# Retention: the gate multiplies the result right after its squares, the root's factor last; one half gets row buffers of its own

## The reference

```python
q, k, v = heads(query, W_Q), heads(key, W_K), heads(value, W_V)      # 16 heads of 32
q, k = xpos(q), xpos(k, downscale=True)
ret = einsum(einsum(q, k) * decay_mask, v)
mu, var = ret.mean(-1), ret.var(-1)                                  # over the 32 of a head
ret = (ret - mu) / sqrt(var + 1e-5)
gate = silu(query @ g_w.T + g_b)
x = layernorm(query + ret * gate @ out_w.T + out_b)
```

## Time and profile before

| | us |
|---|---|
| median of 3 runs | 1864.24 |
| range | 1863.15 to 1866.96 |
| the profiled execution's own time | 1863.1 |
| its span, first to last instruction | 1861.3 |
| TensorE busy over the span | 1696.8 |
| DVE, ACT, POOL busy | 1392.4, 1053.7, 1056.4 |

### The profile page before, as it was taken

How to read it: one execution, slowest core, us unless ns; L and a number is a source line. 1 busy time by engine, 2 the same in 40 slices (tenths; PEclk the granted TensorE clock), 3 DMA queues, 4 the chain that set the end, 5 groups by cost and what they waited for, 6 DMA issues and landing times. The chain is left out here.

```text
span 1861.3 us, 37218 instructions
## 1 busy us (share of the span) xinstructions
PE 1696.8 (91%) x13426; PEld 764.8 (41%) x13426; DVE 1392.4 (75%) x3069; ACT 1053.7 (57%) x1865; POOL 1056.4 (57%) x999
## 2 busy tenths in 40 slices
PE   5898999989999999998787899999999997799897
PEld 2433343433433344333233455545455553344343
DVE  7687756786677866678654977878778777688798
ACT  5346655675556655566642556555465454465587
POOL 4049867687685967869862664645655555000054
PEclk9999999999999999999897999999999999899999
DMA  8302112231113211212224223322232221561085
GB/s 274 116 17 60 55 29 58 70 93 42 24 50 95 88 35 37 74 54 78 86 86 157 70 81 98 112 84 91 85 108 76 75 92 57 189 236 48 23 315 188
DMA packets 125263, 172.27 MB, mean 93 GB/s; under 512 B 24600, under 2 KB 75160, under 8 KB 124184
## 3 DMA queue, kind: packets, MB, share of 16 engines
q1 hardware_dynamic: 119704, 161.37, 27.0%
q10 hardware_dynamic: 5376, 8.52, 1.4%
HBM read 106.38 MB, written 38.14 MB: 78 GB/s over the span
## 5 line engine op out<-in xcount | busy, mean ns | idle before, releaser
L1153 DVE CUSTOM_DVE_ANT_0 a_mx<-a_mx,a_mqk 128x128 f32<-128x128 f32 (+3 forms) x512 | 241.9, 512 | 131.2 <-PE a_mx L1353 130.4
L963 ACT ACTIVATE a_P<-a_mx 128x512 f32<-128x512 f32 (+3 forms) x441 | 199.7, 498 | 148.7 <-PE a_mx L1371 79.7
L1236 POOL TENSOR_TENSOR a_P<-a_P 128x512 f32<-128x512 f32 (+3 forms) x202 | 194.0, 987 | 107.9 <-PE a_o L1383 95.3
L1367 PE MATMUL a_mx<-a_Qs,a_Ks 128*128 128x512 f16 (+3 forms) x768 | 231.2, 334 | 17.3 <-ACT a_P L963 5.5
L1353 PE MATMUL a_mx<-a_Ks,a_Qs 96*128 96x512 f16 (+3 forms) x768 | 227.2, 332 | 10.7 <-DVE a_nm L1153 3.9
L963 ACT ACTIVATE share<-a_mx 128x512 f32<-128x512 f32 (+3 forms) x327 | 145.4, 492 | 107.4 <-PE a_mx L1371 59.6
L1236 POOL TENSOR_TENSOR a_P<-a_P,share 128x512 f32<-128x512 f32 (+3 forms) x199 | 184.3, 955 | 27.9 <-ACT share L963 17.4
L1156 DVE TENSOR_REDUCE a_nm<-a_mx 128x1 f32<-128x512 f32 x256 | 164.7, 684 | 30.9 <-PE a_mx L1353 30.0
L2217 PE MATMUL r_pj<-share,cth 128*128 128x512 f16 x672 | 172.6, 391 | 6.9 <-PEq L123 5.5
L2937 PE MATMUL f_pj<-f_xqT,f_wgu 128*128 128x512 bf16 x704 | 158.3, 381 | 2.3 <-ACT f_sg L2779 2.3
L2217 PE MATMUL r_pj<-r_xTh,share 128*128 128x512 f16 x512 | 157.9, 381 | 2.6 <-DVE r_xTl L2064 1.7
(11 more groups left out here) (294 smaller groups left out, 4027.1 us busy)
## 6 DMA issues: line engine op xcount, KB each, us to landing
x_scratch<-rows SPq DMA_DIRECT2D x60, 256.0 KB, 2.0
rows<-x_scratch SPq DMA_DIRECT2D x56, 256.0 KB, 4.5
lead<-in_xT SPq DMA_DIRECT2D x24, 512.0 KB, 4.6
lead<-in_ctxT SPq DMA_DIRECT2D x38, 256.0 KB, 2.8
h_scratch<-f_h SPq DMA_DIRECT2D x3, 2816.0 KB, 9.2
f_h<-h_scratch SPq DMA_DIRECT2D x3, 2816.0 KB, 14.3
a_Ks<-a_kph SPq DMA_DIRECT2D x256, 32.0 KB, 1.9
a_Qs<-a_qph SPq DMA_DIRECT2D x256, 32.0 KB, 1.9
```

What stands on the lines that cost most here:

```text
L963: act.activation(Pf[pf.at[key]][:, off:512], pb[:, off:512], ACT.Exp).then_inc(p_exp, 1)
L1153: dve.tensor_tensor_reduce(bank_of(it)[:, 0:n], bank_of(it)[:, 0:n], mqk[:, 512 - n:512], 1.0, -3e38, ALU.add, ALU.max, nm[:, col:col + 1] ...
L1236: pool.tensor_tensor(total[:, off:512], total[:, off:512], Pf[pf.at[key]][:, off:512], ALU.add).then_inc(add_pool, 1)
L1367: m = pe.matmul(pb[:, off:512], Ks[s][:, j, kt * P:(kt + 1) * P], Qs[s][:, j, qb * 512 + off:(qb + 1) * 512], start=True, stop=not diag)
```

## The change

1. `zg` is now the multiplication of `r_rt` by the gate. DVE does it (into one of two buffers `r_zt`) as soon as `sq` has read the result and the gate is there. The multiplication by the root's factor `r_rex` comes last, on POOL, in place in `r_zt` (item `z.0`). One multiplication on DVE and one on POOL for each unit, as before.
2. The gate's buffer and R's bank are free after `zg` (R's also needs `sq`), no longer after the last multiplication; the plan's conditions say the same.
3. The last but one half, `AHEAD = (3, 0)`, keeps its rows in four buffers of its own, `r_ahead`. The last half uses `rows`, which half (2, 1) left earlier. Its loads are put 2.1 places earlier in the plan.

```diff
@@ retention_plan
-            put("ACT", ("G", *u), 1.9, out, lambda: was("z", n - 2))
+            put("ACT", ("G", *u), 1.9, out, lambda: was("zg", n - 2))
...
-            put("ACT", ("sq", *u), 0.54, lambda: put("DVE", ("var", *u), 1.3, var), lambda: was("rt", n - 1))
+            put("ACT", ("sq", *u), 0.54, lambda: (done.add(("sq", *u)), put("DVE", ("var", *u), 1.3, var), put(
+                "DVE", ("zg", *u), 0.62, gated, lambda: has(("G", *u)) and was("zl", n - 2))), lambda: was("rt", n - 1))
...
-                "DVE", ("rt", *u), 0.65, rt, lambda: was("zg", n - 1)))))
+                "DVE", ("rt", *u), 0.65, rt, lambda: was("z", n - 1)))))
+
+        def gated():
+            done.add(("zg", *u))
...
-            put("POOL", ("zg", *u), 1.4, gated, lambda: has(("G", *u)))
-
-        def gated():
-            done.add(("zg", *u))
-            put("DVE", ("z", *u), 0.62, z, lambda: was("zl", n - 1))
+            put("POOL", ("z.0", *u), 1.4, z, lambda: has(("zg", *u)))
...
-        pe_item(R, place + 0.4, ("R", *u), 2.3, retained, lambda: was("z", n - 2) and has(
+        pe_item(R, place + 0.4, ("R", *u), 2.3, retained, lambda: was("zg", n - 2) and was("sq", n - 2) and has(
...
+        prior = HALVES[HALVES.index((b, hf)) - (2 if (b, hf) == HALVES[-1] else 1)]
+        loads.append((places[0] - (0.4 if (b, hf) != HALVES[-1] else 2.5), lambda: put(
+            "SP", ("y", *key), 0.5, lambda: after(3.5, landed), lambda: (b, hf) in (HALVES[0], AHEAD) or has(("am", *prior, k), ("st", *prior, k)))))
@@ retention_phase
-    yt = keep.rows
+    ahead = [sb(f"ahead{i}", [P, D], F32) for i in range(4)]
...
+    def rows_of(b, hf, k):
+
+        i = HALVES.index((b, hf))
+        if (b, hf) == AHEAD:
+            return ahead[k], (ahead_in[k], 16), ahead_out[k]
+        return keep.rows[k], (yt_in[k], 16 * (i + 1 if i < len(HALVES) - 1 else i)), x2_out[k]
@@ scalar (G)
-                    w.wait_ge(z_dve, n - 2)
+                    w.wait_ge(zg_dve, n - 2)
@@ vector
-            elif kind == "z":
-                w.wait_ge(zg_pool, n)
-                if n > 1:
-                    w.wait_ge(z_lo, n - 1)
-                dve.tensor_tensor(zt[:, :], ret[n % 2][:, :], gate[n % 2][:, :], ALU.mult).then_inc(z_dve, 1)
+            elif kind == "zg":
+                w.wait_ge(sq_act, n)
+                w.wait_ge(g_act, n)
+                if n > 2:
+                    w.wait_ge(z_lo, n - 2)
+                dve.tensor_tensor(zt[n % 2][:, :], ret[n % 2][:, :], gate[n % 2][:, :], ALU.mult).then_inc(zg_dve, 1)
@@ gpsimd
-            elif kind == "zg":
+            elif kind == "z.0":
                 w.wait_ge(rt_dve, n)
-                w.wait_ge(g_act, n)
-                pool.tensor_tensor(gate[n % 2][:, :], gate[n % 2][:, :], rex[:, :], ALU.mult).then_inc(zg_pool, 1)
+                w.wait_ge(zg_dve, n)
+                pool.tensor_tensor(zt[n % 2][:, :], zt[n % 2][:, :], rex[:, :], ALU.mult).then_inc(z_pool, 1)
@@ tensor (R)
-                    w.wait_ge(z_dve, n - 2)
+                    w.wait_ge(zg_dve, n - 2)
+                    w.wait_ge(sq_act, n - 2)
```

More of the change, by code:

```diff
@@ L1779, in retention_phase @@
     AD = [[sb(f"AD{i}{j}", [P, 512], F32) for j in range(4)] for i in range(2)]
-    sq, sqT, rex, zt = (sb(n, [P, 512], F32) for n in ("sq", "sqT", "rex", "zt"))
+    sq, sqT, rex = (sb(n, [P, 512], F32) for n in ("sq", "sqT", "rex"))
+    zt = [sb(f"zt{i}", [P, 512], F32) for i in range(2)]
     gate = [sb(f"gate{i}", [P, 512], F32) for i in range(2)]
@@ L1887, in sync @@
                 r0, n = b * L + hf * 512 + k * P, num[it]
-                if n > 4:
-                    w.wait_ge(x2_out[k], 16 * ((n - 1) // 4))
-                    w.wait_ge(am_dve, n - 4)
+                i = HALVES.index((b, hf)) - (2 if (b, hf) == HALVES[-1] else 1)
+                if i >= 0 and (b, hf) != AHEAD:
+                    w.wait_ge(x2_out[k], 16 * (i + 1))
+                    w.wait_ge(am_dve, num[("am", *HALVES[i], k)])
                 x1_stored(w)
-                sp.dma_start(yt[k][:, :], x1d[r0:r0 + P, :]).then_inc(yt_in[k], 16)
+                y, (landed, _), _ = rows_of(*key)
+                sp.dma_start(y[:, :], x1d[r0:r0 + P, :]).then_inc(landed, 16)
             elif kind == "lead":
@@ L1914, in sync @@
                 w.wait_ge(tn_act, num[it])
-                sp.dma_start(x2d[r0:r0 + P, :], yt[k][:, :]).then_inc(x2_out[k], 16)
+                y, _, stored_out = rows_of(*key)
+                sp.dma_start(x2d[r0:r0 + P, :], y[:, :]).then_inc(stored_out, 16)
+        for k in range(4):
+            w.wait_ge(ahead_out[k], 16)
         for i in range(2):
@@ L1980, in scalar @@
                 b, hf, g = key
[L1981 removed]
+                w.wait_ge(z_pool, n)
                 if b or hf:
                     w.wait_ge(o_mm, num[("out", *half_before(b, hf), 3)])
[L1984 removed]
+                act.activation(zh[:, g, :], zt[n % 2][:, :], ACT.Copy).then_inc(z_hi, 1)
             elif kind == "fround":
@@ L2011, in scalar @@
                 w.wait_ge(rs_dve, 2 * num[("norm", b, hf, normed_with(b, hf, k)[0])])
-                act.activation(yt[k][:, :], yt[k][:, :], ACT.Identity, bias=mr[:, k:k + 1], scale=rs[:, k:k + 1]
+                y = rows_of(*key)[0]
+                act.activation(y[:, :], y[:, :], ACT.Identity, bias=mr[:, k:k + 1], scale=rs[:, k:k + 1]
                                ).then_inc(tn_act, 1)
@@ L2157, in vector @@
                 w.wait_ge(tn_act, n)
-                dve.tensor_reduce(amax[:, col:col + 1], yt[k][:, :], AXX, ALU.max, apply_absolute_value=True
+                dve.tensor_reduce(amax[:, col:col + 1], rows_of(*key)[0][:, :], AXX, ALU.max, apply_absolute_value=True
                                   ).then_inc(am_dve, 1)
@@ L2206, in gpsimd @@
                 w.wait_ge(const_in, NCONST)
-                w.wait_ge(yt_in[k], 16 * ((n + 3) // 4))
-                pool.tensor_tensor(yt[k][:, :], yt[k][:, :], ob[:, :], ALU.add).then_inc(y_pool, 1)
+                y, landed, _ = rows_of(*key)
+                w.wait_ge(*landed)
+                pool.tensor_tensor(y[:, :], y[:, :], ob[:, :], ALU.add).then_inc(y_pool, 1)
     def tensor(pe):
```

22 lines of the change are left out of this document (11 added, 11 removed).

## The result

The changed kernel takes 1859.27 us (median of 20 runs, 1854.93 to 1863.39), the kernel before 1863.45 in 20 runs beside it. The ratio is 0.9978, 95% interval 0.9970 to 0.9986: 4.2 us faster, where 9.2 were forecast. The profiled execution took 1862.75 us.

What follows compares the result with a forecast made beforehand. It took TensorE, busy 91% of the span, as the bound. -3.9 - 3.4 - 2.1 + 1.7 - 1.5 = -9.2 us took the profiled 1863.1 to 1853.9; with 1.1 for the median, 1855.0, range 1848 to 1866.

Steps and rivals of the forecast that it cites:

- Halves (3, 0) and (3, 1): Retention's last two halves: the sum had no term for the new order there.
- the gain is passed on: Rival: TensorE's removed waits only move to its next ones; 1861.0 us or no gain at all; chance 0.20.
- The four scores: Last unit's scores in (0, 1), (1, 0), (2, 0), (2, 1): shorter waits for the gate, -3.9 us, bounds 0 and 6.0.
- the clock: Low-clock stretches at 1140 and 1210 us, behind two of the scores' stalls, both go: -3.4 us.
- My four terms of the middle: Middle of retention: scores -3.9, clock -3.4, stall in half (0, 0) -2.1, table loads +1.7 us.
- the condition that the change relaxes matters here only through the order: Gate's wait for the multiplication two units earlier: long met, so relaxing it acts only through the plan's written order.
- The stall of 4.18 us: Half (0, 0), TensorE waiting for the last key tile's `lead`: shrinks to about 2.1 us, so -2.1, bounds 0 and 4.18.
- Four table loads: ACT: four more loads of 1.28 us as roots and gates alternate more, mostly hidden; +1.7 us, bounds 0 and 5.1.
- Retention's end: Last unit and first outputs: a DVE multiplication and a table load leave the chain; 1.5 us saved, bounds 1.9 and -0.5.
- own buffers: Row buffers of half (3, 0): cost nothing by themselves, same loads and stores, eight more semaphores to clear.
- Slower: Rival: the earlier multiplication on DVE delays items TensorE waits for, 0.69 us per such unit; +7.8 us, 1872; chance 0.13.
- my signs of being wrong: TensorE's waits from 1075 to 1540 us undiminished, a low-clock stretch in the middle, or a later end relative to the last scores.

Runs made afterwards that it cites:

- e3_late_scores: Changed kernel with A and R of unit (3, 0, 3) placed later in the plan (27.55 and 27.9); 1853.06 us, ratio 0.9946.
- e0_after: The changed kernel run again with no edit; 1859.12 us, ratio 0.9977.
- e5: Kernel before, with `rx` of the third unit behind the last gate and `rt` behind the next `xT` in four halves; 1863.90 us, ratio 0.9992.
- e9: e5 with DVE's last multiplication of the third unit also behind the last unit's decayed scores at the same four places; 1862.32 us, ratio 0.9986.
- e4: Changed kernel, but the gate and R wait for the last multiplication of two units earlier, as before the change; 1862.85 us, ratio 0.9993.
- e1: Changed kernel without the own row buffers of half (3, 0) and the loads' new conditions, only the gate's part; 1858.58 us, ratio 0.9974.
- e7: e3_late_scores with, in (3, 1), the last unit's query moved ahead on POOL, `rt` behind it on DVE, `z` behind the gate on ACT; 1855.02 us.
- e3a: Changed kernel with A and R of (3, 0, 3) at 27.3 and 27.65, so only R goes behind V and the last `xT`; 1857.18 us, ratio 0.9962.
- e12: e7 with, in (3, 0), `rx` of the third unit behind the last gate on ACT and `rt` behind the next `xT` on DVE; 1858.08 us.

## Why the prediction was right and wrong

The forecast was 9.2 us, the measurement 4.2. In pieces the forecast was -7.7 in the middle, nothing in (3, 0)/(3, 1) and -1.5 at the end; the profiles have -6.7, +4.0 and -1.9. By its own steps:

- **Halves (3, 0) and (3, 1): no term, +4.0 us.** This is the step that failed. The new order there stood only as an argument for the rival "the gain is passed on", and the sum had nothing for it. e3_late_scores shows that the order of A, R and `xT` at one unit, with what the plan moves behind it, is the cause. Reading it off was possible: with the piece of order at hand, every product on TensorE that moves ahead of an `xT` on which the next Q hangs has to be priced by the distance of that `xT` from its use.
- **The four scores and the clock, -3.9 and -3.4.** The wait for the gate fell from 6.0 us in four to 0.9 in two, and both low stretches went. The scores did not wait 0.8 us for `xTl`; behind them TensorE waits 0.95 and 1.12 us for the key tile's rotation and 0.20 each for decayed scores. In the middle as a whole, the waits (sum of the brackets between the marks) went from 20.5 to 17.4 us and the lost clock, (1 - PEclk) times the stretch, from 6.8 to 1.7. In e0_after these are 15.9 and 3.4, nearly the same sum. So the clock's term of 3.4 came as forecast; the 1.7 beyond it in the changed kernel's profile lie behind the stall of (0, 0) and do not repeat in e0. My four terms of the middle came to -7.7; it measured -6.7. That they are so near is partly luck. From the last R of one half to that of the next, (0, 1) went from 78.1 us to 73.8 (74.6 in e0), (1, 0), for which I had at least 0.68 + 1.7, from 74.0 to 74.5 (73.4), (2, 0), for which I had 0.95, from 73.3 to 69.9, and (2, 1), for which I had 0.95, from 71.8 to 72.0. And the order at the four scores alone brings nothing that can be told from none (e5, e9). e5 and e9 show that the multiplication must be out of DVE's way; what gives the other 5 us between e9's 461.3 and the changed kernel's 456.3 was not isolated. e4 shows that the sentence "the condition that the change relaxes matters here only through the order" is wrong by 3.6 us. The gate's old wait was long met in the old order, which is all that the earlier trace rows could show.
- **The stall of 4.18 us, -2.1.** It is 2.14 us, as forecast. But the scores ahead of it wait 1.43 us for the state and a query 1.11 for a rotation, which they had not: from the first mark to R of (0, 0, 3) only 1.1 us is gained. The 2.1 us that I let remain was not worked out either: the chain that I named, two passes of 0.69 and an addition of 1.66, is 3.0 us, and how much of it TensorE's work covers I did not say.
- **Four table loads, +1.7.** There are four more. No wait of TensorE in the list names them, and a gate still starts when the load ends (1048.08 + 1.28, gate at 1049.37), so the drain of the Trainium skill, ScalarE: Activation LUTs, section "What ACT_TABLE_LOAD costs", is not to be seen here either. What the four loads cost was not measured by itself and stays open.
- **Retention's end, -1.5; own buffers, 0.** The end is 1.9 us shorter. The split was wrong: the own rows, which I had at nothing by themselves, give 2.1 alone, the gate's part 1.4, and together they give no more than one of them. Both start the last root earlier and bring DVE's first output forward, so they shorten the same way; by how much each does so in the changed kernel was not separated.
- **The rivals.** "Slower" did not come: the middle, with 26 of the 32 units, is shorter. "Passed on" named the mechanism that did come, and the result lies between its 1861.0 and the forecast. Of my signs of being wrong one came, a low stretch of the clock within (3, 0), and one nearly: TensorE's waits between 1075 and 1540 us fell only from 17.0 to 16.2 us.

Which of its new conditions makes the plan write A and R of (3, 0, 3) earlier was not tried. Half (2, 0) became 3.4 us shorter where I had 0.95: its waits fell by 2.2 us (3.6 to 1.4), and eight products less lie between its marks. Four of the projections of keys and values (1.03 us as a row of four) now stand in (3, 0), whose first three units are 1.6 us longer, and four of a row's transposition (0.60) stand ahead of (2, 0).

## What to carry to other kernels

When a condition in a planner is relaxed, look at the whole new order for items that moved ahead of something the next product needs, not only at the places that had stalls; one such place took back 4.0 of 8.6 us here, and two numbers in the plan gave it back (1853.1 us). A wait at an engine that walks a fixed order is removed only if the item next in line at the other engines is ready too: the same move of `rx` brought nothing measurable at four places and cost 4.2 us at a fifth. And a small change is best sized from mark to mark within a profile, with several profiles to see how far a piece repeats: the middle came back within 1.9 us in seven profiles of one order, and the old order's piece in (3, 0)/(3, 1) within 0.02 us in four, while the phase ahead of the first mark moved by 8.

## What the runs showed of the hardware that was not expected

What one stall costs in clock differs between executions of the same order. Between the first two marks, behind the same stall of 2.1 us in half (0, 0), the loss was 1.7 us in the changed kernel, e1 and e7 and 3.4 us in e0, e3, e3a, e4 and e12.

In (3, 0) the clock fell to 1.2 GHz, for a loss of 1.7 us, after waits of 0.59, 0.88 and 0.58 us with short products between them, none of them long, in the changed kernel, e0, e1 and e3a. In e4 the same three waits stood there (0.58, 0.89, 0.58) and the clock stayed at 1.00. It also stayed at 1.00 after the single stall of 1.32 us and after the two of 0.58 and 0.47 in e3_late_scores. So several short waits close together can cost as much clock as a long one, but the same waits need not cost it each time; what decides was not found.
